# Where the input transfers of a four-block kernel are issued, and in what order their parts are waited for

## The reference

```python
x = x + _layernorm(_L0_attn_ref(_layernorm(x, axis=-1), ...), axis=-1)
x = x + _layernorm(_L0_ffn_ref(_layernorm(x, axis=-1), ...), axis=-1)
x = x + _layernorm(_L1_attn_ref(_layernorm(x, axis=-1), ...), axis=-1)
x = x + _layernorm(_L1_ffn_ref(_layernorm(x, axis=-1), ...), axis=-1)
```

## Time and profile before

| | us |
|---|---|
| median of 3 runs (lowest to highest) | 2476.78 (2475.42 to 2477.82) |
| the profiled execution, its own time | 2480.28 |
| span of the profiled execution | 2478.5 |
| PE busy / DVE busy / ACT busy / POOL busy | 1999.3 / 1430.5 / 1140.1 / 630.9 |
| first instruction of `ssm_block` on DVE starts at | 28.27 |
| first matmul (a transpose) starts at | 43.05 |
| first projection starts at | 46.16 |
| `chunks` of batch 0 starts on PE at | 74.14 |

### The profile page before, as it was taken

One profiled execution on the slowest core, in us unless ns is written; L12 is line 12 of the kernel. 1 busy time (PEld: TensorE's weight loads), 2 busy tenths in 40 slices (PEclk: granted clock), 3 DMA queues, 4 the chain that ended last, 5 costly groups with the idle time before them and its releaser, 6 DMA issues. The chain is left out here.

```text
span 2478.5 us, 28184 instructions
## 1 busy us (share of the span) xinstructions
PE 1999.3 (81%) x8474; PEld 1430.8 (58%) x8474; DVE 1430.5 (58%) x3222; ACT 1140.1 (46%) x2757; POOL 630.9 (25%) x1932
## 2 busy tenths in 40 slices
PE   2878788898666687678669666589999999999997
PEld 1544554555554575567557555358657756865774
DVE  3566563232488898899889888333344245335324
ACT  1333232101388898888889888112312221231321
POOL 2322431010244454454444443210010010001000
PEclk9778788999877798789879877899999999999998
DMA  5000000001000000000000000000000000000000
GB/s 211 1 0 0 0 0 0 0 0 51 1 1 1 1 1 1 1 1 1 1 1 1 1 1 1 0 1 1 1 0 10 1 0 10 1 1 0 9 1 9
DMA packets 6593, 19.91 MB, mean 8 GB/s; under 512 B 958, under 2 KB 3966, under 8 KB 5183
## 3 DMA queue, kind: packets, MB, share of 16 engines
q1 hardware_dynamic: 6462, 18.30, 2.0%
HBM read 16.20 MB, written 2.10 MB: 7 GB/s over the span
## 5 line engine op out<-in xcount | busy, mean ns | idle before, releaser
L1273 ACT ACTIVATE mem_arena<-mem_arena,r_shift 128x256 f32<-128x256 f32 x864 | 384.5, 501 | 12.6 <-POOL r_shift L1212 12.4
L1044 DVE BATCH_NORM_STATS2 r_moments<-mem_arena 128x6 f32<-128x512 f32 x576 | 371.0, 684 | 2.0 <-ACT mem_arena L1273 1.7
L1359 PE MATMUL r_bank<-G,r_wT 128*128 128x256 f32 x1024 | 291.0, 447 | 32.4 <-ACT mem_arena L1273 26.8
L1359 PEld LDWEIGHTS r_bank<-G,r_wT 128*128 128x128 f32 x1024 | 227.1, 228 | 80.1 <-issue 43.2
L1815 ACT ACTIVATE e_PT<-e_banks 128x512 f32<-128x512 f32 x160 | 95.5, 597 | 312.0 <-PE e_banks L1955 311.8
L1556 DVE TENSOR_REDUCE e_NM<-e_banks 128x2 f32<-128x1024 f32 (+3 forms) x128 | 105.3, 825 | 223.1 <-PE e_banks L1930 223.1
L1373 PE MATMUL r_bank<-ident,mem_arena 128*128 128x128 f32 x576 | 107.1, 318 | 144.7 <-DVE mem_arena L1060 144.7
L1021 DVE MAX8 r_top<-r_bank 128x8 f32<-128x256 f32 x384 | 152.6, 422 | 83.0 <-PE r_bank L1359 82.3
L1373 PEld LDWEIGHTS r_bank<-ident,mem_arena 128*128 128x128 f32 x576 | 79.7, 164 | 170.7 <-DVE mem_arena L1060 160.4
L1966 PE MATMUL e_banks<-e_PT,e_V 128*128 128x256 f32 (+3 forms) x512 | 172.3, 450 | 0.0
L1359 PE MATMUL r_bank<-G,r_xnT 128*128 128x256 f32 x512 | 130.0, 413 | 27.9 <-ACT mem_arena L1273 23.6
(11 more groups left out here) (308 smaller groups left out, 3978.3 us busy)
## 6 DMA issues: line engine op xcount, KB each, us to landing
w<-in_w SPq DMA_DIRECT2D x3, 1024.0 KB, 13.6
X<-in_x SPq DMA_DIRECT2D x1, 2048.0 KB, 7.5
out_x<-X SPq DMA_DIRECT2D x4, 512.0 KB, 2.9
w_in<-in_w_in SPq DMA_DIRECT2D x1, 1156.0 KB, 8.9
mem_arena<-in_wq SPq DMA_DIRECT2D x1, 1024.0 KB, 17.3
mem_arena<-in_wo SPq DMA_DIRECT2D x1, 1024.0 KB, 19.7
gate<-in_gate SPq DMA_DIRECT2D x1, 1024.0 KB, 4.8
up<-in_up SPq DMA_DIRECT2D x1, 1024.0 KB, 7.0
```

What stands on the lines that cost most here:

```text
L1044: last = dve.bn_stats(moments[:, a.lane, 2 * p:2 * p + 2, :].rearrange("p two c -> p (two c)"), u[a.lane][:, 2 * p:2 * p + 2, :].rearrange ...
L1273: last = act.activation(u[a.lane][:, h, :], u[a.lane][:, h, :] if k else scores[:, h, :], ACT.Relu, bias=shift[:, a.lane, h:h + 1])
L1359: last = pe.matmul(scores[:, h, :], lhs, (G1 if a.first else G2)[:, h, i, :], start=i == 0, stop=i == 1)
```

## The change

SP's transfers move from `load_block` into `ssm_block`. `load_block` keeps POOL's three constants. x is split: 512 rows (`X[:, 0:TPB, :]`) stand in front of all others with the semaphore `s_x`, the other 1536 rows behind w_out with a semaphore of their own, `s_xs`. `LOAD_SSM` is split into `LOAD_SMALL` (vec, ident, tri; `s_small`) and w_in and w_out (`s_ssm`). The waits follow: DVE waits for `s_x` or `s_xs` in `row_stats`, and for `s_small` and the negated `A_log` only after `normed_rows(0)`; POOL no longer waits ahead of `row_rstd(0)`; PE waits for `s_small` ahead of the transposes and for `s_ssm` ahead of the projections. POOL's Hadamard additions wait for `xn_ready` too, that is until DVE has written all normed rows of batch 0.

```diff
-def load_block(nc, T, dram):
+def load_block(nc, T):
     with nc.Block() as block:
-        @block.sync
-        def _(sp):
-            sp.dma_start(T["X"][:], dram["x"]).then_inc(T["s_x"], 16)
-            for name in LOAD_SSM:
-                sp.dma_start(T[name][:], dram[name]).then_inc(T["s_ssm"], 16)
...
@@ ssm_block @@
+        @block.sync
+        def _(sp):
+            sp.dma_start(X[:, 0:TPB, :], dram["x"][:, 0:TPB, :]).then_inc(T["s_x"], 16)
+            for name in LOAD_SMALL:
+                sp.dma_start(T[name][:], dram[name]).then_inc(T["s_small"], 16)
+            for name in LOAD_SSM:
+                sp.dma_start(T[name][:], dram[name]).then_inc(T["s_ssm"], 16)
+            sp.dma_start(X[:, TPB:, :], dram["x"][:, TPB:, :]).then_inc(T["s_xs"], 16)
+            for name in LOAD_FFN:
+                sp.dma_start(T[name][:], dram[name]).then_inc(T["s_ffn"], 16)
...
         @block.vector
         def _(dve):
             dve.memset(conv_in[:, :, 0:DCONV - 1], 0.0)
-            dve.wait_ge(T["s_x"], 16)
-            dve.wait_ge(T["s_ssm"], 16 * len(LOAD_SSM))
-            dve.wait_ge(a_ready, 1)
-            dve.tensor_scalar(neg_a[:], neg_a[:], -1.0, None, ALU.mult)
+
             def row_stats(b):
+                dve.wait_ge(T["s_x"] if isinstance(b, int) and b == 0 else T["s_xs"], 16)
                 for t in range(TPB):
...
             row_stats(0)
             normed_rows(0)
+            dve.wait_ge(T["s_small"], 16 * len(LOAD_SMALL))
+            dve.wait_ge(a_ready, 1)
+            dve.tensor_scalar(neg_a[:], neg_a[:], -1.0, None, ALU.mult)
             steps_and_conv(0)
...
@@ POOL @@
-            pool.wait_ge(T["s_ssm"], 16 * len(LOAD_SSM))
...
             row_rstd(0)
 
+            pool.wait_ge(T["s_small"], 16 * len(LOAD_SMALL))
             pool.wait_ge(T["s_ffn"], 16 * len(LOAD_FFN))
+            pool.wait_ge(xn_ready, 1)
...
@@ PE @@
-            pe.wait_ge(T["s_ssm"], 16 * len(LOAD_SSM))
+            pe.wait_ge(T["s_small"], 16 * len(LOAD_SMALL))
...
             columns(0)
+            pe.wait_ge(T["s_ssm"], 16 * len(LOAD_SSM))
             projections(0, True)
...
-LOAD_SSM = ("vec", "ident", "tri", "w_in", "w_out")
+LOAD_SMALL = ("vec", "ident", "tri")
+LOAD_SSM = ("w_in", "w_out")
```

More of the change, by code:

```diff
@@ L101, in _, with ssm_block @@
                 sp.dma_start(T[name][:], dram[name]).then_inc(T["s_exp"], 16)
-def ssm_block(nc, T):
+def ssm_block(nc, T, dram):
     X, ident, tri, vec, w_in, w_out = (T[n] for n in ("X", "ident", "tri", "vec", "w_in", "w_out"))
@@ L195, in heads @@
             return ap.unsqueeze(2).to_broadcast([ap.shape[0], NH0, P])
+        @block.sync
[8 more added lines that the diff above has]
+                sp.dma_start(T[name][:], dram[name]).then_inc(T["s_ffn"], 16)
+            for name in LOAD_MEM:
+                sp.dma_start(T[name], dram[name]).then_inc(T["s_mem"], 16)
+            for name in LOAD_MOE:
+                sp.dma_start(T[name][:], dram[name]).then_inc(T["s_moe"], 16)
         @block.vector
@@ L420, in _ @@
         def _(act):
-            act.wait_ge(T["s_ssm"], 16 * len(LOAD_SSM))
+            act.wait_ge(T["s_small"], 16 * len(LOAD_SMALL))
             act.activation(neg_a[:], col("A_log"), ACT.Exp).then_inc(a_ready, 1)
@@ L2101, in program @@
     with ExitStack() as keep:
-        for name in ("s_x", "s_ssm", "s_ffn", "s_mem", "s_moe", "s_exp", "s_out"):
+        for name in ("s_x", "s_xs", "s_small", "s_ssm", "s_ffn", "s_mem", "s_moe", "s_exp", "s_out"):
             T[name] = keep.enter_context(nc.semaphore(name))
@@ L2115, in program @@
             T["fly"] = layer0.enter_context(nc.sbuf_tensor("fly", [P, HT, D], F32))
-            load_block(nc, T, dram)
+            load_block(nc, T)
             if upto >= 1:
-                done = ssm_block(nc, T)
+                done = ssm_block(nc, T, dram)
             if upto >= 2:
```

## The result

The changed kernel takes 2453.6 us in the median (2449.65 to 2453.95), the kernel before 2476.1 us in the same session (4 executions each): a ratio of 0.9906, 95% interval 0.9891 to 0.9922. That is 22.5 us faster; 2452.5 us were forecast.

The account below looks back on a forecast made before the run. The first 28 us were taken as bound by issuing 27 transfers before a barrier. Projections 32.95 us earlier, less 8.7 us lost in the convolution, give 24.3 us: 2476.8 - 24.3 = 2452.5 us, range 2443 to 2459.

Parts of the forecast that it names:

- statistics start (512 rows landed): DVE's first statistics in the mixer: start at 5.19 us, when a quarter of x has landed, in place of 29.91 us.
- normed rows, start and length: Batch 0's four normed-row operations on DVE: start at 8.59 us and take 1.37 us, not 9.60 us.
- w_out lands: Transfer queue: with 1.57 MB of x less ahead of it, w_out lands at 9.9 us in place of 12.9 us.
- projections start: First projection of batch 0 on PE: starts at 13.21 us, 32.95 us earlier than before.
- loss of `chunks` against the bare shift: Batch 0's `chunks` on PE: 8.7 us later than the 32.95 us shift alone gives, since POOL's additions delay the convolution.
- What bounds the start: First 28 us: bound by issuing 27 transfers before the first block's barrier, not by data, which landed long before.
- The wait for the normed rows: POOL's additions wait for `xn_ready`, so batch 0's normed rows take 1.37 us; 8.2 us of the 32.95 us.
- Additions over the convolution: POOL's additions and DVE's convolution operations alternate; convolution ends at 49.0 us, 12.3 us late, 8.7 us of it lost.
- The start of the additions: POOL's additions wait for `s_ffn`, complete when `had` lands at 21.3 us; DVE's copy holds POOL to 22.4 us.
- No cost: Rival: POOL's additions cost the convolution nothing, the whole 32.95 us shift stays, 2443.8 us; chance 0.13.
- slower start: Rival: first rows or instructions come late, DVE's small operations meet POOL's additions; with 5 us, 2458.7 us; chance 0.13.
- the fetches of instructions: Rival, slower than before: two instruction fetches in the chain, behind full transfer queues, lose 39.4 us, 2491.9 us; chance 0.03.

## Why the prediction was right

The steps, against the trace of the changed kernel:

| step | forecast | trace after |
|---|---|---|
| SP's first issue | 1.42 | 1.22 |
| statistics start (512 rows landed) | 5.19 | 5.18 |
| normed rows, start and length | 8.59, 1.37 | 8.51, 1.38 |
| w_out lands | 9.9 | 12.05 |
| projections start | 13.21 | 13.25 |
| first addition starts | 21.3, held to 22.4 | 23.73 |
| last addition ends | 38.9 | 39.92 |
| convolution ends | 49.0 | 48.19 |
| loss of `chunks` against the bare shift | 8.7 | 7.9 |
| `m_xd` starts | 51.7 | 50.91 |

- **What bounds the start.** The barrier behind 27 issues did. The run with the place of issue alone shows it: 20.1 of 25.05 us. Splitting x gave 4.0 us more, splitting the groups and waits 1.0.
- **The wait for the normed rows.** I credited `xn_ready` with keeping the additions off the normed rows (8.2 us). The rows got their 1.38 us, but the run without the wait shows that it does nothing here. In the prediction's own times the additions could not have started before 21.3 us, 11 us after the normed rows end. The step's size was right, its cause was not: the moved issue does it.
- **Additions over the convolution.** The loss was put at 8.7 us, from POOL and DVE alternating. Against the bare shift it is 7.9 us (49.09 - 13.25 less the 27.98 us from first projection to `chunks` before); against the run without additions, whose projections ran faster (12.42 us in place of 13.50 before), 8.9. The additions hold the convolution back and memsets do not: shown by the run with memsets. A handover hides part of the short operation, as I took from the earlier trace rows: 14.3 us of additions took 16.2 us (23.73 to 39.92), where five convolution operations in full would have made it 18.
- **The start of the additions.** This term was mis-sized: `had` landed 2.3 us later than I put it, and w_out 2.1 us later, 1.2 us before the projections needed it. I let the split cost the later transfers nothing, and put the rate at that of the earlier trace rows. Between 3 and 7 us the changed kernel moved 308 GB/s, and with x in one piece 389; the earlier trace rows has 422. With x in one piece the additions start at 21.2 us, with the split at 23.7: SP spends 3.28 us on issuing the three transfers w1, w3, w2, which took it 1.46 us before and 1.47 us with x in one piece. It did no harm, since almost two convolution operations were done by then, ahead of the first addition.
- **The rivals.** "No cost" would have shown `chunks` at 41.2 us; "slower start" and the fetches of instructions would have shown gaps ahead of 13 us; there are none. The remaining scatter, up to 6 us in the mixer, was not in my range's reasoning; it would have been a reason for a wider one.
- **How much of the agreement is luck.** `chunks` was forecast 24.3 us earlier and came 25.05 us earlier: that is the mechanism. That the median lies 1.1 us from the forecast is in part luck. The gain is 22.5 us in the medians and 27.0 us in the profiled executions, of which 1.9 us arose in the mixer's later stretch (291.7 us before, 289.8 after), and one kernel's executions scatter by more than those 1.1 us.

## What to carry to other kernels

Here a block that only issued transfers cost its whole issue time, since a barrier stood behind it: issue within the first block that computes, and put in front only what its first operation needs. A piece cut off the front can make what lies behind it land later, and a semaphore shared by two transfers waits for the later one: look at both when the order changes. When work of POOL is moved, ask which of DVE's operations it comes to lie beside: if both read SBUF and DVE has two inputs there (or is a plain `tensor_scalar`), each of DVE's operations can wait for most of one of POOL's, which hurts most where DVE's are short. And read a gain where it arises: some 8 us at the start can drown in the scatter of a later stretch.

## What the runs showed that I had not expected

- A short operation pays as much as a long one: 0.17 us became 2.0 to 2.2 us beside an addition of 2.35, and a convolution operation of 0.75 us at most 2.83 us, while a reciprocal (one input) on the same 16 columns kept 0.25 us beside one.
- Splitting x slows the queue: the last transfer that the additions wait for lands 2.5 us later with two pieces than with one (23.6 and 21.1 us), though the bytes are the same.
- With identical instructions and an identical start, the mixer's stretch lasted 289.8 and 296.1 us, at mean granted clocks of 0.79 and 0.75.
